# Mean layers: where the extra columns are added, and when the last three quads are summed

## What is computed

```python
src, dst = (edge_index[0], edge_index[1])
n = x.shape[0]
deg = jax.ops.segment_sum(jnp.ones(src.shape[0], x.dtype), dst, num_segments=n)
inv_deg = (1.0 / jnp.maximum(deg, 1.0))[:, None]

def sage_conv(h, Wl, b, Wr):
    agg = jax.ops.segment_sum(h[src], dst, num_segments=n) * inv_deg
    return agg @ Wl + b + h @ Wr
h = jax.nn.relu(sage_conv(x, W_l0, b0, W_r0))
h = jax.nn.relu(sage_conv(h, W_l1, b1, W_r1))
return sage_conv(h, W_l2, b2, W_r2)
...
x = _layernorm(x + _L2_gnn_ref(x, edge_index, L2_gnn_W_l0, L2_gnn_b0, L2_gnn_W_r0, L2_gnn_W_l1, L2_gnn_b1, L2_gnn_W_r1, L2_gnn_W_l2, L2_gnn_b2, L2_gnn_W_r2), axis=-1)
```

## Time and profile before

| what | us |
| --- | --- |
| median of three runs | 7239.66 |
| the profiled execution | 7241.22 |
| its span | 7239.4 |
| PE busy (76%) | 5528.3 |
| POOL busy (69%) | 4967.1 |
| DVE busy (65%) | 4732.1 |
| ACT busy (31%) | 2265.0 |

### The profile page before, as it was taken

How to read it: one execution, slowest core, us unless ns; L and a number is a source line. 1 busy time by engine, 2 the same in 40 slices (tenths; PEclk the granted TensorE clock), 3 DMA queues, 4 the chain that set the end, 5 groups by cost and what they waited for, 6 DMA issues and landing times. The chain is left out here.

```text
span 7239.4 us, 119762 instructions
## 1 busy us (share of the span) xinstructions
PE 5528.3 (76%) x30345; PEld 4159.5 (57%) x30345; DVE 4732.1 (65%) x20294; ACT 2265.0 (31%) x5973; POOL 4967.1 (69%) x5179
## 2 busy tenths in 40 slices
PE   4675667777777767777767777789898996888887
PEld 3442344556656556656656566666665665666665
DVE  7985678466666456666546666664545556888887
ACT  1044443211114311113411112543333333454554
POOL 5777764677777577777577777657475673777774
PEclk7688888788888778888878888899999997998898
DMA  9433352577777467777567777667576762222222
GB/s 306 133 79 87 78 114 51 164 207 208 207 211 220 140 193 209 209 210 221 159 179 208 208 205 209 185 185 208 159 207 179 209 205 73 56 57 56 56 57 53
DMA packets 911701, 1151.31 MB, mean 159 GB/s; under 512 B 143234, under 2 KB 676290, under 8 KB 911106
## 3 DMA queue, kind: packets, MB, share of 16 engines
q1 hardware_dynamic: 689296, 673.54, 30.7%
q0 software_dynamic: 202464, 461.07, 23.8%
q10 hardware_dynamic: 19346, 9.66, 0.5%
HBM read 882.09 MB, written 261.74 MB: 158 GB/s over the span
## 5 line engine op out<-in xcount | busy, mean ns | idle before, releaser
L498 POOL DMA_INDIRECT G<-table_kv,idx x2496 | 2381.6, 954 | 956.0 <-issue 744.6
L1708 DVE SCALAR_TENSOR_TENSOR sums<-ramp,place,bank 128x128 f32<-128x128 f32 x2496 | 718.6, 343 | 1180.1 <-PE bank L1627 1084.3
L1617 PE MATMUL bank<-ident,G 128*128 128x128 f32 x2496 | 649.2, 337 | 708.0 <-DMA G<-table_kv,idx 701.1
L2140 POOL DMA_INDIRECT G<-table_h,src_idx x864 | 823.0, 953 | 480.5 <-issue 256.6
L1596 ACT COPY slab<-bank 128x512 f32<-128x512 f32 x624 | 364.0, 583 | 2293.4 <-PE bank L1617 2293.2
L498 POOL DMA_INDIRECT G<-table_h,idx x832 | 828.9, 996 | 301.4 <-issue 228.2
L1627 PE MATMUL bank<-qT,slab 128*128 x4992 | 906.9, 339 | 99.6 <-issue 82.2
L1617 PEld LDWEIGHTS bank<-ident,G 128*128 128x128 f32 x2496 | 382.7, 164 | 928.1 <-DMA G<-table_kv,idx 885.5
L1627 PEld LDWEIGHTS bank<-qT,slab 128*128 128x128 f32 x4992 | 793.9, 242 | 197.8 <-issue 196.8
L1839 DVE TENSOR_SCALAR OH<-ramp,place,weight 128x128 f32<-128x128 f32 x2076 | 721.7, 357 | 13.8 <-issue 6.9
L2126 PE MATMUL bank<-sums,qT 128*128 128x418 bf16 (+1 forms) x3528 | 672.2, 333 | 33.4 <-DVE same L2049 12.3
(11 more groups left out here) (351 smaller groups left out, 9582.8 us busy)
## 6 DMA issues: line engine op xcount, KB each, us to landing
stash<-G SPq DMA_DIRECT2D x312, 512.0 KB
sums<-stash SPq DMA_DIRECT2D x624, 256.0 KB
sums<-adjacency SPq DMA_DIRECT2D x294, 522.5 KB
adjacency<-same SPq DMA_DIRECT2D x49, 1184.0 KB
same<-adjacency SPq DMA_DIRECT2D x90, 522.5 KB
G<-table_kv,idx POOLq DMA_INDIRECT x2496
sums<-adjacency SPq DMA_DIRECT2D x48, 408.0 KB
table_kv<-G SPq DMA_DIRECT2D x72, 256.0 KB, 3.3
```

Source lines behind the costliest of these rows:

```text
L498: pool.indirect_dma_start(G[:, s, 0:width], None, tab, bass.IndirectOffsetOnAxis(ap=idx[:, s:s + 1], axis=0)).then_inc(c_gather[s].sem, 16)
L1617: ins = pe.transpose(bank[q % 2][:, (s % QUAD) * P:(s % QUAD + 1) * P], G[:, s, 0:D], ident[:])
L1708: ins = dve.scalar_tensor_tensor(scratch[:, s, :], ramp[:], place[:, n * QUAD + s:n * QUAD + s + 1], bank[2 + q % 2][:, s * P:(s + 1) * P] ...
L2140: pool.indirect_dma_start(G[:, s, 0:D], None, table[l], bass.IndirectOffsetOnAxis(ap=src_idx[:, DENSE + t:DENSE + t + 1], axis=0)).then_in ...
```

## The change

- The extra columns are added to `xT` instead of `agg`. `xT` is set to zero by seven memsets of 896 columns at the beginning of `dve_sums`. Ten columns go with a quad instead of eight, quads 4 to 58, and they stand among the four window additions. A window addition waits for window additions alone, an extra column for extra columns alone.
- With quads 59 to 65 DVE adds `xT` to `agg` in seven parts of 896 columns.
- Three quads fewer are spread over the product (`TAIL_QUADS`); PE does quads 69, 70 and 71 behind its last step, and half 1 is added ahead of quad 69. Half 0 is added ahead of quad 34.
- In the third layer the residual comes in four pieces into `slab`, `G`'s second half and `dst_part`: 16 blocks, 16 blocks and one block loaded at the end of the first 17 steps' loads, 16 blocks where all of it was loaded before. They are added with quads 12, 16, 17 and 34.

```diff
@@ -2129,7 +2131,9 @@
         def quads_by(n):
-            return 2 + (n - GROUPS) * (RUN_QUADS - 2) // (STEPS - GROUPS) if n > GROUPS else 0
+            return 2 + (n - GROUPS) * (RUN_QUADS - 2 - TAIL_QUADS) // (STEPS - GROUPS) if n > GROUPS else 0
+
+        TAIL_QUADS = 3
@@ -2162,46 +2166,41 @@
                 ins = pe.matmul(bank[SUM_BANKS[q % 3]][:, k * P:(k + 1) * P], G[:, s, 0:D], OH[:, s, :], start=True, stop=True)
             ins.then_inc(c_rows.sem, 1)
-        EXTRAS_A_QUAD = 8
+        EXTRAS_A_QUAD = 10
         EARLY_QUADS = quads_by(FIRST_STEPS)
-        assert (RUN_QUADS - EARLY_QUADS) * EXTRAS_A_QUAD >= DENSE
-        EXTRA_ADDS = DENSE + 2 * NODE_BANKS
+        EXTRA_QUADS = -(-DENSE // EXTRAS_A_QUAD)
+        PLACED_QUAD = EARLY_QUADS + EXTRA_QUADS
+        PLACED_PARTS = 7
+        PLACED = NP // PLACED_PARTS
+        assert PLACED_QUAD + PLACED_PARTS <= RUN_QUADS and PLACED * PLACED_PARTS == NP
+        RESIDUAL_QUADS = (EARLY_QUADS + 8, EARLY_QUADS + 12, EARLY_QUADS + 13, EARLY_QUADS + 30)
+        FIRST_RESIDUALS = 3
+        WHOLE_ADDS = PLACED_PARTS + 2 * NODE_BANKS
         def dve_sums(l):
-
-
-            n = [0, 0]
-
-            def after_adds():
-                dve.wait_ge(c_added.sem, c_added.at(n[0]))
-
-            def after_extra():
-                if n[1]:
-                    dve.wait_ge(c_extra.sem, c_extra.at(n[1]))
-
-            extras_left = [DENSE]
-
-            def add_extras(k):
-                after_adds()
-                done = DENSE - extras_left[0]
-                extras_left[0] -= k
-                for d in range(done, done + k, QUAD):
-                    windows = window_at(DVE, d, QUAD)
-                    for j in range(QUAD):
-                        after_extra()
-                        w = agg[:, bass.ds(windows[j], 1)]
-                        dve.tensor_tensor(w, w, extra[:, d + j:d + j + 1], ALU.add).then_inc(c_extra.sem, 1)
-                        n[1] += 1
+            last = []
+
+            def after_last():
+
+                for sem, n in last:
+                    dve.wait_ge(sem, n)
+
+            def next_is(c, n):
+                last[:] = [(c.sem, c.at(n))]
+
+            wholes = [0]
+
+            def add_whole(w, part):
+                after_last()
+                dve.tensor_tensor(w, w, part, ALU.add).then_inc(c_whole.sem, 1)
+                wholes[0] += 1
+                next_is(c_whole, wholes[0])
             def add_half(half):
-                after_adds()
                 dve.wait_ge(adj_used.sem, adj_used.at(FIRST_STEPS + (half + 1) * BLOCKS))
                 for c in range(NODE_BANKS):
-                    w = agg[:, bass.ds(chunk_start(DVE, half * NODE_BANKS + c), BANK_COLS)]
-                    after_extra()
-                    dve.tensor_tensor(w, w, bank[c][:, 0:BANK_COLS], ALU.add).then_inc(c_extra.sem, 1)
-                    n[1] += 1
-                after_extra()
+                    add_whole(agg[:, bass.ds(chunk_start(DVE, half * NODE_BANKS + c), BANK_COLS)], bank[c][:, 0:BANK_COLS])
+                after_last()
                 dve.sem_inc(adj_read.sem, 1)
             def keep_extras():
@@ -2211,36 +2210,70 @@
                 ins.then_inc(adj_read.sem, 1)
                 dve.wait_ge(adj_read.sem, adj_read.at(1))
+            def place_extra(d, node):
+
+                dve.wait_ge(c_extra.sem, c_extra.at(X_PARTS + d))
+                w = xT[:, bass.ds(node, 1)]
+                dve.tensor_tensor(w, w, extra[:, d:d + 1], ALU.add).then_inc(c_extra.sem, 1)
+
+            for part in range(X_PARTS):
+                dve.memset(xT[:, part * PLACED:(part + 1) * PLACED], 0.0).then_inc(c_extra.sem, 1)
             half_quads = quads_by(FIRST_STEPS + BLOCKS) - 2
             for q in range(RUN_QUADS):
                 if q == EARLY_QUADS:
                     keep_extras()
                 if q == half_quads:
                     add_half(0)
+                if q == RUN_QUADS - TAIL_QUADS:
+                    add_half(1)
+                done = max(0, q - EARLY_QUADS) * EXTRAS_A_QUAD
+                extras = range(done, min(DENSE, done + EXTRAS_A_QUAD) if q >= EARLY_QUADS else done)
                 windows = window_at(DVE, DENSE + q * QUAD, QUAD)
-                dve.wait_ge(c_rows.sem, c_rows.at(q + 1))
-                after_extra()
+                places = dict(zip(extras, window_at(DVE, done, len(extras)) if extras else ()))
                 for k in range(QUAD):
-                    if n[0]:
-                        after_adds()
+                    for d in extras[len(extras) * k // QUAD:len(extras) * (k + 1) // QUAD]:
+                        place_extra(d, places[d])
+                    if k == 0:
+                        dve.wait_ge(c_rows.sem, c_rows.at(q + 1))
+                    after_last()
                     w = agg[:, bass.ds(windows[k], P)]
                     dve.tensor_tensor(w, w, bank[SUM_BANKS[q % 3]][:, k * P:(k + 1) * P], ALU.add).then_inc(c_added.sem, 1)
-                    n[0] += 1
-                if q >= EARLY_QUADS and extras_left[0]:
-                    add_extras(min(EXTRAS_A_QUAD, extras_left[0]))
-                if l == 2 and q == half_quads + 4:
-                    dve.wait_ge(residual_in.sem, residual_in.at(16))
-                    dve.tensor_tensor(hT[:], hT[:], xT[:], ALU.add)
-            add_half(1)
-
+                    next_is(c_added, q * QUAD + k + 1)
+                part = q - PLACED_QUAD
+                if part in range(PLACED_PARTS):
+                    if part == 0:
+                        dve.wait_ge(c_extra.sem, c_extra.at(X_PARTS + DENSE))
+                    at = slice(part * PLACED, (part + 1) * PLACED)
+                    add_whole(agg[:, at], xT[:, at])
+                if l == 2 and q in RESIDUAL_QUADS:
+                    r = RESIDUAL_QUADS.index(q)
+                    dve.wait_ge(residual_in.sem, residual_in.at(16 * max(r + 1, FIRST_RESIDUALS)))
+                    home, b0, nb = residual_rows(r)
+                    dve.tensor_tensor(nodes_h[:, b0:b0 + nb, :], nodes_h[:, b0:b0 + nb, :], home, ALU.add).then_inc(residual_added.sem, 1)
+            after_last()
             dve.tensor_tensor(agg[:, 0:BANK_COLS], agg[:, 0:BANK_COLS], agg[:, NODES:], ALU.add)
+
+        SLAB_BLOCKS = MASK_COLS // D
+
+        def residual_rows(r):
+
+            b0 = (0, SLAB_BLOCKS, BLOCKS - 1, 2 * SLAB_BLOCKS)[r]
+            slab_rows = slab[:, 0:SLAB_BLOCKS * D].rearrange("p (b d) -> p b d", d=D)
+            home = (slab_rows, G[:, :, D:2 * D], dst_part[:, 0:D].unsqueeze(1), slab_rows)[r]
+            return home, b0, home.shape[1]
+
+        assert SLAB_BLOCKS == SLOTS and 3 * SLAB_BLOCKS + 1 == BLOCKS
+
+        def sp_residual(r):
+            home, b0, nb = residual_rows(r)
+            sp.dma_start(home, table[0][b0 * P:(b0 + nb) * P, :].rearrange("(b p) d -> p b d", p=P)).then_inc(residual_in.sem, 16)
...
@@ -2315,6 +2348,8 @@
                     pe_dense(n)
                     for q in range(quads_by(n), quads_by(n + 1)):
                         pe_sum_quad(q)
+                for q in range(quads_by(STEPS), RUN_QUADS):
+                    pe_sum_quad(q)
         norm_passed()
         sums_passed()
@@ -2329,10 +2364,14 @@
                 @block.sync
                 def _(_e):
                     sp_sage_weights(l)
-                    sp_adjacency(0, FIRST_STEPS + BLOCKS // 2)
+                    sp_adjacency(0, FIRST_STEPS)
                     if l == 2:
-                        sp.wait_ge(own_rows.sem, own_rows.at(GROUPS))
-                        sp.dma_start(xT[:].rearrange("p (b d) -> p b d", d=D), table[0].rearrange("(b p) d -> p b d", p=P)).then_inc(residual_in.sem, 16)
+                        for r in range(FIRST_RESIDUALS):
+                            sp_residual(r)
+                    sp_adjacency(FIRST_STEPS, FIRST_STEPS + BLOCKS // 2)
+                    if l == 2:
+                        sp.wait_ge(residual_added.sem, residual_added.at(1))
+                        sp_residual(FIRST_RESIDUALS)
                     sp_adjacency(FIRST_STEPS + BLOCKS // 2, STEPS)
                 @block.gpsimd
```

7 lines of the change are left out of this document (5 added, 2 removed).

## The result

The changed kernel takes 7201.27 us (median of 5 runs, 7197.6 to 7214.3), the kernel before 7240.96 in the same job (5 runs, 7233.92 to 7249.64): ratio 0.995, 95% interval 0.9939 to 0.9961. It is faster by 0.5%, 40 us, inside the range; the 7187 forecast wanted 53.

What follows compares the result with a forecast made beforehand. DVE, three quads behind PE at the product's end, was taken as the bound, with POOL the hidden second limit. Gains of 15.6, 15.4 and 21.7 us in the three layers, 52.7 off 7239.66, gave 7187 us; range 7173 to 7209.

Steps and rivals of the forecast that it cites:

- rival (a): Mean layers: POOL becomes the bound and its stops reach the layer's end; 40.9 us gained, 7199 us; chance 0.18.
- product: First layer, step 17 to the product's end: 323.7 us, with PE's waits for gathers taken as gone.
- The tail: First layer, from the product's end to PE's next work: 14.0 us, where 23.2 was taken before.
- The load of ten: DVE's quads with ten extras: one load of ten registers costs 0.45 us, between bounds of 0.38 and 3.8.
- 0.7 of slack: DVE's quads with extras: 4.2 us against PE's 4.94, leaving 0.7 us in each of 55 quads.
- my own rule on what a lost cover costs: DVE's quads with extras: without PE's cover, each 0.1 us in a quad costs 5.5 us a layer.
- The zeroes: Layer start: seven memsets take 5.4 us, as good as hidden in the first; step 17 1.9 late in second and third.
- The gathers: POOL beside DVE's part additions: additions with both inputs in SBUF stop POOL, 3.5 us a layer.
- The third layer: Residual in the third layer: loads still cost 1.5 us, POOL loses 1.6 for each of three additions; 21.7 us gained.
- (c): DVE's quads with extras: the load of ten costs 3.8 us, a quad 7.55; 7561 us; chance 0.03.
- (b): DVE's additions: the chains don't interleave, 5.5 us a quad, DVE the bound again; 7216 us; chance 0.07.
- (d): Mean layers: nothing stops POOL or DMA and the memsets hide; 62.3 us gained, 7177 us; chance 0.10.

Runs made afterwards that it cites:

- Cut loads: The changed kernel with the ten extras' column numbers loaded in pieces of at most four that begin at multiples of four: 7202.26 us, ratio 0.9942.
- the kernel with three mends: The changed kernel with extras by turns 8 and 12 a quad, zeroing memsets spread, first four quads at their old places: 7191.47 us, ratio 0.9928.

## Why the prediction was right, and where it was not

The sign, the range and the shape of the end came out; the gain did not, 33.4 in the layers (40 by the medians) against 52.7. That the total lies in the range is owed to its reach up to rival (a), not to the sum: two of the signs that it named for being wrong came, quads on DVE over 4.95 apart with no release by PE and a register load over 0.5, and the product ended 331.5 behind step 17, not 323 to 326. By its own terms:

| term, three layers | predicted | measured |
|---|---|---|
| start: quad 0 to step 17 | +3.8 | +6.0 |
| product | -32.1 | -9.3 |
| tail | -24.4 | -30.2 |
| sum | -52.7 | -33.5 |

- **The tail, right.** 14.0 was summed for DVE's chain; it took 13.9, 13.3, 13.3. The 1.4 and 2.9 that I added for a late quad 71 in the first and third layers did not come.
- **The load of ten, the step that failed.** The sum took 0.45, by the nearest row, a load of four, "as it is one instruction". It took 1.07 and 2.30, in the mean 1.7. The rest of the DVE quad was right: 4.2 - 0.45 + 1.7 = 5.45 for the 5.25 measured. That put DVE over PE's 4.94, so the "0.7 of slack" was -0.3, and my own rule on what a lost cover costs held in kind, though three banks hid two thirds of it: 55 x 0.3 = 17 us of lag became 5.4 us a layer. Cut loads gave back 14.9 of the 22.8 by which the product term was off; most of the rest is the next point.
- **The restart of step 17, not seen.** I carried a slow start for the second half alone. With step 17 later by 0.7 to 2.7, PE idles 2.5 or 4.5 us ahead of it instead of 1.8, and its first ten matmuls take 3.5 instead of 1.94. In PE's rows by stretch the granted clock is 0.60 over that step and 0.50 over the first step of the second half, against 1.00 in the stretches between:

```profile
4808.20:4812.50 4.30, 4.30 (x15) 2.04 (x16) 0.32 (x2) 0.00 (x0) 3.25 (x4) 0.60 0.36 124
4814.00:4850.00 36.00, 36.00 (x225) 22.99 (x224) 16.20 (x95) 13.73 (x38) 27.16 (x30) 1.00 0.73 220
4973.80:4979.00 5.20, 5.18 (x16) 2.42 (x17) 2.42 (x14) 0.00 (x0) 3.21 (x4) 0.50 0.19 55
```

  (columns: stretch, length, busy time and count of PE, PEld, DVE, ACT, POOL, granted clock, DMA share, GB/s). 0.50 is the lower level, 1.2 GHz; 0.60 is mostly that. With its quad step 17 takes 5.2, 6.1 and 5.7 in the three layers where it took 3.6: 6.4 us in all. With 1.8 of idle time ahead of it, before and in the kernel with three mends, step 17 ran at 2.4 GHz throughout; with 2.5 it went either way, slower in nine layers of the runs and at full speed in two.
- **The zeroes, right in kind.** 1.9 in the second and third layers was exact (13.1 less 11.2); the seven take 6.45 and not 5.4, as they stand 0.94 apart; so the exact 1.9 is in part luck. The 0.7 beside it came from quad 3's place, which I had read past: the order at that place moves it one step.
- **The gathers, right in kind, too high.** 3.5 a layer was taken for the part additions; POOL's longer issues sum to 2.6, 2.4 in the first two layers. The Trainium skill (SBUF — State Buffer, "SBUF: two separate sides") says that a DVE instruction with two SBUF inputs and a GpSimd operation that reads SBUF exclude each other for a whole instruction. The runs agree: issues of up to 1.85 beside additions of 1.09, and 0.96 at most in the first two layers once these were gone. The longest stop, 0.9, is shorter than the addition.
- **The third layer.** Its excess over the others, 10 us in the product, vanished, which the prediction put at 1.5 left. PE's wait for adjacency rows is gone. What the residual still costs is POOL's: 5.6 us, visible once POOL is the bound.
- **The rivals.** (a) gave the number, 7199, for the wrong reason: POOL was not yet the bound, though no more than 0.5 us from it. (c) named the right step, but at 3.8 and slower; the truth, 1.7 in the mean, lay between its price and mine. (b) and (d) are out: the chains interleave, and things do stop.

Open stays what POOL's drain waits for in the 7.57 us after the last gather issue; the rows show when it ends and not why.

## What to carry to other kernels

Price a register load by its pieces, not by the instruction: for 4-byte values in SBUF begin it at a multiple of four, take multiples of four, and look for "issue" gaps that alternate. A small excess on a buffered engine stays hidden for dozens of rounds and then costs its full rate, so look at how the distance between producer and consumer grows, not at the waits alone. And where a change makes one end of a stage shorter, work out the other engines' ends, with what they need to leave the block: here POOL's last gather plus 7.85 us left a rearrangement of DVE's work worth 0.5 us. The view of timelines leaves out records like DRAIN; asked for the barrier's own line, the trace shows who came last.

## What the runs showed of the hardware

- A register load on DVE's queue is priced by how its values lie: ten 4-byte values cost 1.07 us from a multiple of four and 2.30 from two beyond one, twelve from a multiple of four 0.85.
- Two chains of dependent additions on DVE that wait on different counters do interleave: 0.13 to 0.21 from one chain's start to the other's, where one chain's own steps are 0.29 and 0.42 apart.
- POOL's drain at a block's end finished 7.56 or 7.57 us after its last gather issue in all 39 mean layers of the 13 profiled executions. PE's next work came 7.85 us after that issue, 8.15 in the first layer, in the twelve layers in which DVE was through 1.7 to 3.2 ahead of PE, and never sooner in any.
- Seven memsets of 896 columns in a row: 0.805 each by the trace, 0.94 from one to the next.
